# A vision tower on one Trainium2 core: the work between the last attention projection and the first expert in another order

## The reference

```python
h = h + _L1_attn_ref(_layernorm(h, axis=-1), ...)       # ends with out @ Wo + bo
h = h + _L1_ffn_ref(_layernorm(h, axis=-1), ...)
# _L1_ffn_ref: xf = the normed rows, E = 64 experts, K = 6, CAP = 128
scores = jax.nn.softmax(xf @ gate_w.T, axis=-1)
_, idx = jax.lax.top_k(scores + gate_b, K)
xb = jnp.zeros((E, CAP, D), xf.dtype).at[se, pos].set(xf[tok], mode='drop')
h = jax.nn.silu(jnp.einsum('ecd,eid->eci', xb, w1)) * jnp.einsum('ecd,eid->eci', xb, w3)
yb = jnp.einsum('eci,edi->ecd', h, w2)
y = jnp.zeros_like(xf).at[tok].add(contrib * wf[:, None])
z = jax.nn.silu(xf @ ws1.T) * (xf @ ws3.T) @ ws2.T      # the shared expert
return (y + z).reshape(shape)
```

## Time and profile before

| | us |
|---|---|
| runs shown | 669.1, 666.92, 668.16; median 668.16 |
| profiled execution: span / its own time | 669.1 / 671.06 |
| PE busy | 523.7 (78%) |
| DVE busy | 444.2 (66%) |
| ACT busy | 370.1 (55%) |
| POOL busy | 233.4 (35%) |
| mean granted clock of TensorE | 0.889 of 2.4 GHz |

### The profile page before, as it was taken

One profiled execution on the slowest core, in us unless ns is written; L12 is line 12 of the kernel. 1 busy time (PEld: TensorE's weight loads), 2 busy tenths in 40 slices (PEclk: granted clock), 3 DMA queues, 4 the chain that ended last, 5 costly groups with the idle time before them and its releaser, 6 DMA issues.

```text
span 669.1 us, 9764 instructions
## 1 busy us (share of the span) xinstructions
PE 523.7 (78%) x3178; PEld 443.0 (66%) x3182; DVE 444.2 (66%) x928; ACT 370.1 (55%) x899; POOL 233.4 (35%) x235
## 2 busy tenths in 40 slices
PE   3944954257545979999999998597999999998945
PEld 3723843023323979999999886585888888787834
DVE  5949997999998256444554612475787887776516
ACT  1637645255445657667767543344677777676600
POOL 2021001023424310111121102247677777777710
PEclk9975978576865889999999999797999999999969
DMA  8960000008000000000000001001677777777466
GB/s 278 382 239 0 1 0 0 0 9 302 18 1 0 13 12 25 25 24 25 24 1 1 1 1 48 21 26 43 186 226 225 228 210 204 221 214 198 124 247 229
DMA packets 44053, 67.43 MB, mean 101 GB/s; under 512 B 11149, under 2 KB 27142, under 8 KB 43876
## 3 DMA queue, kind: packets, MB, share of 16 engines
q1 hardware_dynamic: 36836, 64.62, 30.4%
q0 software_dynamic: 7168, 2.20, 1.8%
HBM read 66.81 MB, written 17.72 MB: 126 GB/s over the span
## 4 chain that ended last, share of the span: by engine, by line
PE 44%; DVE 29%; DMA 9%; issue 7%; POOL 5%; ACT 5%; SPq 1%; POOLq 0%; DVEq 0%; ACTq 0%
PE ps L711 6%; PE ps L712 5%; PE ps L713 5%; PE ps L922 5%; PE ps L880 4%; PE ps L1058 4%; DMA region<-x_rows,region 4%; DVE region L1700 3%; DMA region<-y_rows 2%; PE ps L911 2%; PE ps L894 2%; POOL y_rows L678 2%; PE ps L787 2%; DVE region L1644 2%; PE ps L1033 2%
## 5 line engine op out<-in xcount | busy, mean ns | idle before, releaser
L1700 DVE TENSOR_TENSOR region<-ps,region 32x136 f32<-32x136 f32 x128 | 38.1, 297 | 73.9 <-PE ps L880 72.4
L711 PE MATMUL ps<-nTh,high 128*128 128x272 f32 (+2 forms) x248 | 75.3, 304 | 12.4 <-ACT region L1277 8.8
L669 POOL DMA_INDIRECT region<-x_rows,region x64 | 71.3, 1114 | 20.7 <-issue 14.0
L678 POOL DMA_INDIRECT y_rows<-region x64 | 70.8, 1106 | 20.3 <-issue 11.0
L712 PE MATMUL ps<-nTl,high 128*128 128x272 f32 (+2 forms) x248 | 73.2, 295 | 0.0
L632 POOL COPY region<-region 32x544 f32<-32x544 f32 x32 | 26.1, 815 | 134.1 <-DVE region L1719 132.6
L1058 PE MATMUL ps<-region 88*128 88x256 f32 x256 | 65.7, 379 | 0.0
L1830 DVE TENSOR_TENSOR w_low<-region,high 128x704 fp32r<-128x704 f32 x64 | 56.9, 889 | 9.0 <-ACT high L1366 8.9
L711 PEld LDWEIGHTS ps<-nTh,high 128*128 128x128 f32 (+2 forms) x248 | 47.4, 191 | 15.2 <-ACT region L1277 10.3
L713 PE MATMUL ps<-nTh,pairs_low 128*128 128x272 f32 x192 | 56.3, 293 | 0.0
L1366 ACT ACTIVATE high<-region 128x704 fp32r<-128x704 f32 x64 | 49.9, 780 | 0.0
(11 more groups left out here) (247 smaller groups left out, 1377.9 us busy)
## 6 DMA issues: line engine op xcount, KB each, us to landing
region<-moe_w SPq DMA_DIRECT2D x64, 352.0 KB, 3.8
region<-moe_w SPq DMA_DIRECT2D x64, 176.0 KB
y_rows<-zrow SPq DMA_DIRECT2D x1, 6528.0 KB, 25.5
region<-y_rows SPq DMA_DIRECT2D x8, 768.0 KB, 9.7
region<-wqkv SPq DMA_DIRECT2D x8, 384.0 KB, 3.0
region<-ffn_w SPq DMA_DIRECT2D x2, 1024.0 KB, 8.3
region<-patches SPq DMA_DIRECT2D x3, 384.0 KB, 8.3
region<-patches SPq DMA_DIRECT2D x1, 1152.0 KB, 10.7
```

The lines of the kernel that those rows point to most:

```text
L669: nc.gpsimd.indirect_dma_start(out=xb[m8], out_offset=None, in_=x_rows, in_offset=bass.IndirectOffsetOnAxis(ap=sloti[:, m8:m8 + 1], axis=0 ...
L678: nc.gpsimd.indirect_dma_start(out=y_rows, out_offset=bass.IndirectOffsetOnAxis(ap=sld[m8], axis=0), in_=yb[m], in_offset=None, bounds_che ...
L711: nc.tensor.matmul(out, parts_a[0], parts_b[0], start=first, stop=False)
L1700: last = V.tensor_tensor(sc[r, s0:s0 + 8, 0:T].rearrange("p (a b) t -> p a b t", a=4), ps[r, 4:8, 0:4 * GW].rearrange("p a (b h t) -> p a ...
```

## The change

- The five groups of transposes of the last norm get banks 0, 1, 5, 4, 5. The first two are transposed ahead of the last Wo tile, the third right after it. ACT and DVE take their parts in the same order.
- The shared expert goes by tokens: `shared(k)` is chunk k // 3, part k % 3. From k = 3 on its results go through banks 0 and 1. The first three come before the gate's logits.
- `second_shared(t)` reads hsh itself, uses banks 2 to 4, and all nine tiles stand ahead of the loop, between the steps of the gate and after the last shared product. DVE's sums go with them; htile, its copies and its semaphore are gone. The first expert product waits for all nine sums.
- ACT runs one element of Exp after the second copy of logits.
- POOL clears the expert buffers and makes `spread_e` and `code` when the first Wo tile is done, ahead of its two powers of the norm. After nine shared products it issues gathers 0 and 1, then product 9, gather 2, product 10, gather 3, product 11, gather 4, and then the loop.
- The step that spreads the groups waits for the table before in place of the shared sum.

```diff
@@ ln_bank
+            if k == 3:
+                return (0, 1, 5, 4, 5)[g]
             return 4 + g % 4 if k == 2 else g % 2
@@ POOL
-            ln(3, 0)
-            ln(3, 1)
-            pool.wait_ge(s_proj, NT)
+            pool.wait_ge(s_proj, 1)
...
+            ln(3, 0)
+            ln(3, 1)
             pool.wait_ge(s_xbz, 12)
...
-            for k in range(3 * CH):
-                ic, q = k // CH, k % CH
+            def gated_shared(k):
+
+                q, ic = k // 3, k % 3
...
+            for k in range(9):
+                gated_shared(k)
             pool.wait_ge(s_xrow, 16 * (NT + 2))
...
             def pool_step(n, b, m8):
-                if 0 <= n + 5 < E:
+                if 5 <= n + 5 < E:
                     gather(n + 5, b + (m8 + 5) // EB, (m8 + 5) % EB)
...
+            gather(0, 0, 0)
+            gather(1, 0, 1)
+            for k in range(9, 3 * CH):
+                gated_shared(k)
+                gather(k - 7, 0, k - 7)
             run_steps(pool_step)
@@ PE
+            def shared(k):
+
+                q, ic = k // 3, k % 3
+                a, b = SIC[ic]
+                for u in range(2):
+                    n = 2 * k + u
+                    bank = n % 4 if n < 6 else n % 2
+                    if n >= 4:
+                        pe.wait_ge(s_sh_ev, n - 3 if n < 6 else n - 1)
...
+            def second_shared(t):
+
+                pe.wait_ge(s_hsh, 3 * -(-min((t + 1) * P, N) // CW))
+                need(pe, s_h4, t - 2)
+                for ic in range(3):
+                    w = SIC[ic][1] - SIC[ic][0]
+                    mm = nc.tensor.matmul(ps[0:rows(t), 2 + t % 3, 0:D], hsh[0:w, ic, t * P:t * P + rows(t)],
+                                          shared_w2[0:w, ic, :], start=(ic == 0), stop=(ic == 2))
+                mm.then_inc(s_z, 1)
...
                     pe.wait_ge(s_h3, t - 3)
+                    if t == NT - 1:
+                        ln(3, 0, 2)
                     project(t, 0, HP)
+            ln(3, 2, 3)
+            pe.wait_ge(ln_low[3], 2)
+            pe.wait_ge(s_slo, 1)
+            shared(0)
+            shared(1)
+            ln(3, 3)
+            shared(2)
             for q in range(CH):
...
+            second_shared(0)
+            second_shared(1)
+            for k in range(3, 6):
                 shared(k)
+            pe.wait_ge(s_glg, 1)
+            second_shared(2)
             pe.wait_ge(s_mc, 3)
             pe.wait_ge(s_sel, 1)
...
             mm.then_inc(s_before, 1)
-            for k in range(6, 8):
-                shared(k)
+            second_shared(3)
+            shared(6)
+            shared(7)
...
-            for k in range(8, 10):
+            shared(8)
+            second_shared(4)
+            place_slots(0)
+            second_shared(5)
+            for k in range(9, 3 * CH):
                 shared(k)
...
+            for t in range(6, NT):
+                second_shared(t)
@@ pe_step
+                if n == 0:
+                    pe.wait_ge(s_h4, NT)
...
-                    elif n >= 0:
-                        pe.wait_ge(s_h4, b + 1)
                     else:
-                        pe.wait_ge(s_tab, 1)
+                        pe.wait_ge(s_tab, 2 * b + 3)
...
-                if m8 == 2 and 0 <= n < E:
-                    pe.wait_ge(s_htile, b + 1)
-                    if n < E - EB:
-                        pe.wait_ge(s_tab, 2 * b + 3)
-                    second_shared(b, 0, 2)
-                if m8 == 3 and 0 <= n < E:
-                    second_shared(b, 2, 3)
-                if n == E - 2:
...
-                    second_shared(NT - 1, 0, 3)
@@ ACT
             squares(3, 0, 7)
             norm(3, 0)
+            squares(3, 7, 8)
+            ln(3, 0, 2)
+            squares(3, 8, NT)
+            ln(3, 2, 3)
+            shared_halves(0)
+            norm(3, 1)
+            shared_halves(1)
+            ln(3, 3)
+            shared_halves(2)
+            for q in range(CH):
+                act.wait_ge(s_lq, q + 1)
+                nc.scalar.activation(lgT[:, q * CW:(q + 1) * CW], ps[0:E, 6 + q % 2, 0:CW], ACT.Copy).then_inc(s_lgT, 1)
+                if q == 1:
+                    nc.scalar.activation(gsum[:, 0:1], mhalf[:, 0:1], ACT.Exp)
+            act.wait_ge(s_glg, 1)
+            nc.scalar.activation(lg, lg, ACT.Exp).then_inc(s_gexp, 1)
+            for k in range(3, 3 * CH):
+                shared_halves(k)
@@ DVE
+                if t == NT - 2:
+                    low_parts(3, 0, 2)
-            ln_norm(3, 1)
-            low_parts(3, 0, 3)
+            ln_variance(3, 1)
+            low_parts(3, 2, 3)
+            ln_finish(3, 1)
             low_parts(3, 3, len(groups))
...
             V.tensor_tensor(lg, logits, bc(gmx, 2, E), ALU.subtract).then_inc(s_glg, 1)
+            shared_sum(0)
...
             V.tensor_copy(nth16, nth).then_inc(s_xpk, 1)
+            shared_sum(1)
+            shared_sum(2)
...
+            shared_sum(3)
             dve.wait_ge(s_rep, 3)
...
             widen_slots(0)
+            shared_sum(4)
             keep_slots(0, 0)
             keep_slots(0, 1)
+            for t in range(5, NT):
+                shared_sum(t)
```

More of the change, by code:

```diff
@@ L1009, in _ @@
                 spread_groups(5 + c, 0, c)
-            for k in range(8, 10):
-                shared(k)
-            place_slots(0)
-            for k in range(10, 3 * CH):
-                shared(k)
-            def second_shared(t, lo, hi):
-                for ic in range(lo, hi):
-                    w = SIC[ic][1] - SIC[ic][0]
-                    mm = nc.tensor.matmul(ps[0:rows(t), 6, 0:D], htile[0:w, ic, 0:rows(t)], shared_w2[0:w, ic, :],
-                                          start=(ic == 0), stop=(ic == 2))
-                if hi == 3:
-                    mm.then_inc(s_z, 1)
+            shared(8)
[3 more added lines that the diff above has]
+            for k in range(9, 3 * CH):
+                shared(k)
+            for t in range(6, NT):
+                second_shared(t)
             def pe_step(n, b, m8):
@@ L1318, in _, with shared_halves @@
                 move(n, n % 2)
-            squares(3, 0, 7)
-            norm(3, 0)
-            squares(3, 7, NT)
-            ln(3, 0, 3)
-            norm(3, 1)
-            for q in range(CH):
-                if q == 2:
-                    ln(3, 3)
-                act.wait_ge(s_lq, q + 1)
-                nc.scalar.activation(lgT[:, q * CW:(q + 1) * CW], ps[0:E, 6 + q % 2, 0:CW], ACT.Copy).then_inc(s_lgT, 1)
-            act.wait_ge(s_glg, 1)
-            nc.scalar.activation(lg, lg, ACT.Exp).then_inc(s_gexp, 1)
-            for k in range(3 * CH):
-                m = SIC[k // CH][1] - SIC[k // CH][0]
+            def shared_halves(k):
+                m = SIC[k % 3][1] - SIC[k % 3][0]
                 if k >= 3:
@@ L1366, in act_step @@
                     nc.scalar.activation(w13_h[k % 2], w13[k], ACT.Copy).then_inc(s_w1h, 1)
-                if m8 == 1 and 0 <= n < E or n == E - 3:
-                    t = b if m8 == 1 else NT - 1
-                    if t == 0:
-                        act.wait_ge(s_hsh, 3 * CH)
-                        act.wait_ge(s_xbz, 13)
-                    need(act, s_z, t)
-                    w = rows(t) if isinstance(t, int) else P
-                    nc.scalar.activation(htile[:, :, 0:w], hsh[:, :, t * P:t * P + w] if isinstance(t, int) else
-                                         hsh[:, :, bass.ds(t * P, P)], ACT.Copy).then_inc(s_htile, 1)
             run_steps(act_step)
@@ L1741, in _, with shared_sum @@
                     ln_finish(3, 0)
-            ln_norm(3, 1)
-            low_parts(3, 0, 3)
+                if t == NT - 2:
[3 more added lines that the diff above has]
+            ln_finish(3, 1)
             low_parts(3, 3, len(groups))
+            def shared_sum(t):
+                r = slice(0, rows(t))
+                dve.wait_ge(s_z, t + 1)
+                V.tensor_tensor(h[r, t, :], ps[r, 2 + t % 3, 0:D], h[r, t, :], ALU.add).then_inc(s_h4, 1)
             dve.wait_ge(s_logit, 1)
```

53 lines of the change are left out of this document (15 added, 38 removed).

## The result

| | before | after |
|---|---|---|
| runs, median | 668.55 | 677.94 |
| lowest and highest | 666.92, 669.1 | 675.95, 680.2 |
| profiled execution, span / its own time | 669.1 / 671.06 | 678.1 / 680.2 |

The changed kernel is slower: the ratio is 1.0146, with a 95% interval of 1.0109 to 1.0182, or 9.4 us between the medians of four runs each. I had forecast +6.5. The profiled execution lies 2.3 us above the median of its kernel, as that of before did by 2.9 (2.5 against the median of this comparison), so the two spans can be set against each other: +9.0.

The account below looks back on a forecast made before the run. POOL's row of 120 gathers and puts was taken to bound the loop. +7.7 (later loop start) - 0.9 - 0.3 = +6.5 us, giving 674.7 us against the median of 668.16; range 666.5 to 678.0.

Parts of the forecast that it names:

- the routing between T0 and gather 0: From logits at DVE (427.9) to gather 0 at 450.8: of the 4.75 us gained, 2.5 left at the first slot table.
- T0: Moment DVE starts on the gate's logits after Wo: 427.9 against 432.7 us, a gain of 4.75.
- the slow issues of the loop: POOL's longer gathers and puts among the loop's 120: left as they are, no more than 3 us either way.
- The loop is POOL's: Expert loop: POOL's 120 gathers and puts set the pace, 2.84 us per expert, while PE needs less.
- the early Exp: Before the last two logits copies on ACT: one Exp with a table load, 1.5 us.
- Gathers ahead of product 11, the wait and the fallen clock: Before second_shared(6): gathers 0 to 3 delay product 11, PE waits 3 us, three tiles take 6.2 us instead of 3.9.
- the head: Everything ahead of the loop: product 0 at 469.5, 7.7 us later, with gather 8 and put 0 keeping their distance.
- The -0.9 and -0.3: Loop time regained where POOL waited for PE: 0.9 us between gathers 8 and 12, some 0.3 at the end.
- PE bounds the loop: Rival in the expert loop: the 11.6 us of PE come out in full, 664.2 us; chance 0.12.
- A gather hardly holds POOL: Rival: POOL's spans overlap what follows, product 11 ready at 457.4, loop is PE's, 660.5 us; chance 0.03.
- DVE held by the early memsets: Rival at the first Wo tiles: DVE's add waits for POOL's memsets, PE up to 2.8 us, 677.5; chance 0.05.
- The start moves but little: Rival ahead of the loop: no wait for product 11, clock up, +2.7 or +1.2 us; chance 0.12.

Follow-up runs that it names:

- second pair: The kernel before and the changed kernel, both unchanged, each run and profiled once more on one chip: spans 663.5 and 672.7 us.

## Why the prediction was right in direction and short in size

Two terms of the sum were mis-sized: the routing between T0 and gather 0, by 2.7 us, and the slow issues of the loop, which I had put at nothing and which came to 3.7 to 3.9 us. Other terms erred the other way, so that the forecast is no further off is partly luck.

*The loop is POOL's: right.* The kernel without the second product is as fast as the one with it, and PE's saved time appears as waits for gathers, 12.7 us. Only where they lie was wrong: I had put them from the start of the loop, some 0.3 us a step; from 491 to 512 us PE still has no gap, and the waits come later.

*T0: 0.5 us too late.* 31.62 against 32.13, and 31.6 in every execution with this head and the early Exp. The added load of Silu's table and the early Exp are where I had them. Of the 1.5 us for the early Exp, only 0.57 stood in the path. The row shows no drain behind a load: the load of 1.28 us at 423.60 ends at 424.88 and the next ACTIVATE starts at 424.89. The Trainium skill, "ScalarE: Activation LUTs", section What ACT_TABLE_LOAD costs, has a drain of 1380 ns there, by which T0 would have been later; the measurement speaks against it here.

*Routing, the first step that failed: T0 to gather 0 took 25.6 us, not 22.85 (450.75 less 427.9).* I had priced shared(3) to (5) at 4.5 us and product 5 at 3.03 us behind its start. The second products of tiles 0 and 1 were through a little early, shared(3) beginning at T0 + 2.4 and not 2.6. But shared(5) began at T0 + 6.94 where I had 5.6, as the tables had to go back to Silu, and that load began only at T0 + 3.6: PE waits 1.07 us for it. In the kernel before, where the load lay right behind Exp, PE waited 0.86 us for it too, and I had left that row out of the price. And product 5 met DVE's scan and lasted 1.66 us instead of 0.78: it was ready 3.86 us behind the start of shared(5), and PE went on 0.15 us later. The trace of the kernel before has such a product at 442.00, which I overlooked. These are 1.34 + 0.83 + 0.15 = 2.3 us, by which second_shared(2) is late: T0 + 10.95, not 8.6. The counting began at T0 + 12.4, not 9.95, and the rest of the chain to gather 0 took 13.2 us against 12.85. This term was mis-sized by 2.7 us. The causes are read from the traces; no run takes the wait or the meeting away.

*Gathers ahead of product 11, the wait and the fallen clock: right, but for the moment of the fall.* 7.5 us for gathers 0 to 3 and three products (8.1, since a product follows a gather at once and a gather a product after 0.16 us), PE's wait 2.5 us (3), 5.9 us for three tiles (6.2), 4.2 us to product 0 (4.4). I had the clock at 0.50 in the wait itself; it was 1.00 there and fell during the first of the three tiles. The kernel with the gathers last, where PE waits 1.33 us and the clock stays at 1.00, shows that these are causes and not company: it gains 2.85 us at product 0. Together with T0 the head is +8.85 where I had +7.7, as -0.5 + 2.7 - 1.0 = +1.2.

*The loop's own time: the second mis-sized term.* The -0.9 and -0.3 came as worked out, -1.2 and -0.9 us in two pairs. But for "the slow issues among the 120 I leave as they are" the two pairs gave +3.9 and +3.7 us. I had bounded them at 3 us either way and put nothing in the sum. What makes an issue slow is shown, its meeting w_low; why the changed kernel had more of it in both pairs stays open, and scatter can do it.

*The sum, put right.* Head +8.85, stretch +2.6, tail -1.65, ahead of Wo -0.8: +9.0 instead of +6.5. The last two are scatter: in the second pair the tail has the other sign, +1.6. With its +7.9 and +2.85, head and loop alone give +10.8, and the medians' +9.4 lies below both pairs' head and loop and above my sum.

*The rivals.* PE bounds the loop: false, by the kernel without second products. A gather hardly holds POOL: false, issues are 1.33 us apart. DVE held by the early memsets: false; DVE's additions take 0.42 us each beside them, from 394.95 on. The start moves but little: false, gather 8 is 7.9 and 8.85 us later.

## What to carry to other kernels

When an engine's issues bound a loop, work moved out of the loop from another engine buys nothing and costs its full length where it lands (some 12 us at product 0 for 11.6 us of work); the gain here (0.6%) came from the reordered head with the second product left in the loop. Ask of every wait that an edit adds what it does to the clock behind it, and of every table switch who waits for it. A DVE operation with two operands in SBUF beside POOL's DMA issues is worth splitting in two, by 0.3 to 0.5% in the three kernels where it was tried, one of them clear of the noise; four pieces gave no more. Ask also of each product on POOL that something waits for what DVE does beside it.

## What the runs showed of the hardware

- POOL's indirect DMA of 128 rows holds the engine for 1.02 us, and the next follows after 0.31 us: 1.33 us each, 159.8 us for 120 in the kernel with the short w_low.
- An issue that begins while DVE subtracts two SBUF operands is held until 0.9 us behind the end of the subtraction and lasts up to 1.72 us, where more than 0.2 us of the subtraction were left; one that began before it is not lengthened (at most 1.04 us). The excess over 120 issues is 12.9 us with one piece of 0.89 us, 6.7 with two and 2.75 with four (second product in the loop), and 0.01 in the changed kernel with the operation cut to 16 columns. In the kernel with short w_low none of DVE's other operations, which mostly have an operand in PSUM, lengthens an issue. The Trainium skill, "SBUF — State Buffer", section SBUF: two separate sides, says that a DVE operation with two SBUF inputs and a GpSimd operation that reads SBUF exclude each other for the whole of the one that was first. The traces agree for DVE before POOL. The other way round they agree for POOL's arithmetic (in the kernel with the second product in the loop a w_low at 451.76, begun beside a product of halves from 451.66 to 452.43, lasts 1.43 us) and not for its DMA issues: 41 w_low of the changed kernel that begin beside one last 0.888 us in the mean, the 23 others 0.892. I had used it in the prediction for the early memsets alone and not for the issues of the loop, where it was worth more.
- The same meeting lengthens arithmetic on POOL: 1.66 us instead of 0.78 for a product beside DVE's scan, and 1.69 in the kernel before.
- Exp's table load ran ahead of the wait of its activation (424.37, Exp at 426.85), while Silu's ran only when PE had delivered (430.16). Why the two differ is open.
- Behind a wait of PE of 2.3 us after dense work the clock stayed at 1.00 in five executions and fell to 0.50 in one. Behind the wait of 2.5 us ahead of the last three second products it fell in all five executions that have it, each time when PE was already multiplying again; behind 1.33 us in the same place it stayed. Over product 0 of the experts it was 0.50 in one execution of the changed kernel and 1.00 in the next. The lower clock cost 1.3 us behind the first wait and 0.9 in the last place.
